# An attention layer's edge loop on one core: three product blocks per slot in place of four, and other PSUM banks

## What is computed

```python
w1 = rbf @ W_rbf
m1_s, m1_v = _cg_tp(msg_s, msg_v, y0, y1, ...)        # product 1
a = leaky(m1_s @ W_alpha).reshape(e, H, AS_);  a = sum(a * alpha_dot, -1)
ex = exp(a - amax[dst]);  alpha = ex / (den[dst] + 1e-16)
val_s = m1_s @ Ws_val
val_v = einsum('ecx,cd->edx', m1_v, Wv_val)
val_v = val_v * sigmoid(val_s @ Wg)[..., None];  val_s = sigmoid(val_s)
m2_s, m2_v = _cg_tp(val_s, val_v, y0, y1, ...)        # product 2
hs = m2_s @ Ws_vlin;  hv = einsum('ecx,cd->edx', m2_v, Wv_vlin)
agg = segment_sum(alpha * concat([hs, hv]), dst)
# _cg_tp: out_s = [w*s*y0, w*dot(v, y1)/sqrt3]
#         out_v = [(w*s)[:, :, None] * y1[:, None, :], w*v*y0, w*cross(v, y1)/sqrt2]
```

## Time and profile before

| | us |
|---|---|
| median of 3 runs | 13186.02 (13185.72 to 13264.55) |
| the profiled execution | 13248.87, its span 13246.9 |
| attention loop in that span | about 8588 to 13165 |
| one turn in the steady part | 10.00 on average |

### The profile page before, as it was taken

How to read it: one execution, slowest core, us unless ns; L and a number is a source line. 1 busy time by engine, 2 the same in 40 slices (tenths; PEclk the granted TensorE clock), 3 DMA queues, 4 the chain that set the end, 5 groups by cost and what they waited for, 6 DMA issues and landing times. The chain is left out here.

```text
span 13246.9 us, 282237 instructions
## 1 busy us (share of the span) xinstructions
PE 10905.0 (82%) x70500; PEld 7225.5 (55%) x70501; DVE 8435.5 (64%) x29911; ACT 4988.2 (38%) x15104; POOL 8742.7 (66%) x12926
## 2 busy tenths in 40 slices
PE   5454453588887999996999956599999999999998
PEld 2000000366664555554666622288888888888886
DVE  7555553499973334433332369588888888888886
ACT  0000000266541222221111100177777777777775
POOL 3777777466655567743777745277777777777775
PEclk9999999999987799985555568699999999999998
DMA  4101100133223233322333356100000000000000
GB/s 154 28 25 25 28 25 19 37 68 68 68 50 66 60 72 74 75 53 57 82 82 82 82 107 117 32 20 20 20 20 20 20 20 20 20 20 20 20 20 21
DMA packets 964724, 635.56 MB, mean 48 GB/s; under 512 B 702351, under 2 KB 886629, under 8 KB 960972
## 3 DMA queue, kind: packets, MB, share of 16 engines
q0 software_dynamic: 257120, 382.51, 11.7%
q1 hardware_dynamic: 691340, 204.27, 8.4%
q10 hardware_dynamic: 15776, 43.25, 0.8%
HBM read 543.06 MB, written 86.47 MB: 48 GB/s over the span
## 5 line engine op out<-in xcount | busy, mean ns | idle before, releaser
L1124 POOL DMA_INDIRECT l1s_node_rows<-node_table,l1s_edge_rows x1216 | 1236.0, 1016 | 655.1 <-issue 316.0
L1124 POOL DMA_INDIRECT l2s_node_rows<-node_table,l2s_edge_rows x1216 | 1152.5, 948 | 653.7 <-issue 351.8
L1209 PE MATMUL l1s_p_outer<-l1s_edge_by_node,l1s_node_rows 128*32 128x64 f32 (+2 forms) x14592 | 1248.9, 275 | 110.7 <-DMA l1s_node_rows<-node_table,l1s_edge_rows 94.0
L461 PE MATMUL rank<-onehot,lower_h 128*128 128x418 f16 x812 | 429.7, 529 | 1035.8 <-DVE onehot L437 966.2
L744 POOL DMA_INDIRECT l_source_rows<-node_table,l_edge_rows x928 | 939.8, 1013 | 437.3 <-issue 278.1
L1209 PE MATMUL l2s_p_outer<-l2s_edge_by_node,l2s_node_rows 128*64 128x40 f32 (+1 forms) x4864 | 1039.2, 345 | 152.8 <-DMA l2s_node_rows<-node_table,l2s_edge_rows 149.2
L1209 PEld LDWEIGHTS l2s_p_outer<-l2s_edge_by_node,l2s_node_rows 128*64 128x64 f32 (+1 forms) x4864 | 837.3, 233 | 549.9 <-issue 356.5
L1209 PEld LDWEIGHTS l1s_p_outer<-l1s_edge_by_node,l1s_node_rows 128*32 128x32 f32 (+2 forms) x14592 | 771.9, 132 | 668.9 <-issue 494.5
L474 POOL DMA_INDIRECT rows_by_src<-row_s,pos_i x812 | 846.6, 1043 | 416.4 <-issue 416.4
L1971 POOL DMA_INDIRECT l_source_rows<-node_table,l_edge_rows x914 | 891.1, 975 | 317.6 <-issue 244.4
L474 POOL DMA_INDIRECT rows_by_dst<-row_d,pos_i x812 | 845.0, 1041 | 267.3 <-issue 267.3
(11 more groups left out here) (504 smaller groups left out, 29142.2 us busy)
## 6 DMA issues: line engine op xcount, KB each, us to landing
l_xv_by<-h_turned_l SPq DMA_DIRECT2D x120, 320.0 KB, 10.6
l_source_rows<-node_table,l_edge_rows POOLq DMA_INDIRECT x1842
l_xs_by<-h_turned_l SPq DMA_DIRECT2D x40, 640.0 KB
rows_by_src<-pad_rows_s ACTq DMA_DIRECT2D x23, 1026.0 KB
l1s_edge_rows<-rows_by_src SPq DMA_DIRECT2D x304, 76.0 KB, 2.3
l2s_edge_rows<-rows_by_src SPq DMA_DIRECT2D x304, 76.0 KB, 2.5
l1s_node_rows<-node_table,l1s_edge_rows POOLq DMA_INDIRECT x1216
l2s_node_rows<-node_table,l2s_edge_rows POOLq DMA_INDIRECT x1216
```

The lines of the kernel that those rows point to most:

```text
L461: nc.tensor.matmul(rank[:, b, 0:BINS], K["lower_h"][:, :], onehot[:, b, :], start=True, stop=False)
L1124: pool.indirect_dma_start(xg[q][:, s, :], None, table, bass.IndirectOffsetOnAxis(ap=pay[q][:, s, S_DST:S_DST + 1].bitcast(U32), axis=0)).t ...
L1209: ins = nc.tensor.matmul(p_o[rows, j % RING, col:col + n], xg[q][:, s, lhs], rhs(eh[q % RING][:, s, :, :]), start=True, stop=True, skip_gr ...
```

## The change

Both products keep three blocks of 128 per slot in place of four. Block 0 holds the scalar outputs (96) and the third axis' share of one vector part (32 columns, the last third of the dot, which is no longer added on DVE but by the matmul, with the weight rows repeated). Block 1 holds the 64 scalars once, unscaled by `y1`, and the first two axes of `v*y0`; block 2 holds its third axis and the cross product of all three axes. The weights `w_v` and `w_hv` become [128, 2, 128]: 32 output columns for the projected scalar part, 96 for the three axes. The scalar part is multiplied by `y1` after the projection, on DVE (`spread`, `val_sum`; `head_spread`, `head_sum`), which the projection's linearity permits.

- PE: six transposes in place of eight, twice; per slot two 128-column matmuls in place of three of 96 columns, for values and for heads. `front_turn` is moved ahead of the transposes of `G_`. The values' matmuls now wait for this turn's `acc_done`, the heads' for `tanh_done`, the sums' for `val_made`.
- ACT: twelve scalings by `y1` go; copies have 384 columns; `gate` (tanh + 1), `sg` (tanh + 1, into `G_`) and four scalings by `y0` come. After `logits_done` the order is now alphas, tanh, gate, front copies, and only then the copies of `G_`.
- DVE: `us` goes straight into `F`; dots have two axes and one addition less; four spread and sum operations, and the head weighting in three pieces come. The order at the start of the turn is new.
- POOL: one small copy of `y1` more (`axis_kept`).
- PSUM: transposes and vector heads share two banks, logits and scalar heads one, values and node sums one.
- Set-up: 56 weight loads in place of 40.

The diff, cut to its core:

```diff
--- before.py
+++ after.py
@@ weights
-            n_loads, LOADS = [], 40
+            n_loads, LOADS = [], 56
@@ cross() on POOL
-                        TT(free(out[:, 0, 1, MS:MS + 1], [PT, PAIR], [P, 3], [1, CV]), there[:, :, :, :], back[:, :, :, :], ALU.subtract).then_inc(m[done], 1)
+                        TT(out[:, :, AT_X:PT].rearrange("p s (i c) -> p s i c", i=3), there[:, :, :, :], back[:, :, :, :], ALU.subtract).then_inc(m[done], 1)
@@ tensor
-                            for n in ("a_done", "a_scaled", "a_crossed"):
+                            for n in ("a_done", "a_crossed"):
                                 wait(n, -1)
-                            wait("g_copied", -1)
                             for s in range(PAIR):
-                                for c in range(4):
+                                for c in range(BLOCKS):
                                     ins = nc.tensor.transpose(...)
                                 ins.then_inc(m["f_turned"], 1)
                             wait("max_taken", 0, 1)
                             masked(1, prev2)
-                            wait("val_made", -1)
+                            wait("acc_done")
                             for s in range(PAIR):
                                 wait("f_copied", 0, s + 1)
...
-                                for i in range(3):
-                                    ins = nc.tensor.matmul(p_a[:, s, D:256], f_t[s][:, (i + 1) * P:(i + 2) * P], w_v[:, i, :], start=i == 0, stop=i == 2)
+                                for c in range(2):
+                                    ins = nc.tensor.matmul(values[:, s, :], f_t[s][:, (c + 1) * P:(c + 2) * P], w_v[:, c, :], start=c == 0, stop=c == 1)
                             ins.then_inc(m["logits_done"], 1)
+                            wait("a3_copied", -1)
+                            wait("hot_made")
+                            front_turn(ahead_u)
...
-                            wait("acc_done")
+                            wait("tanh_done")
                             for s in range(PAIR):
                                 wait("g_copied", 0, s + 1)
...
@@ scalar
                             wait("logits_done")
-                            wait("b_done", -1)
-                            nc.scalar.activation(slope[:, :, :], p_a[:, :, 0:CS], ACT.Copy, scale=0.2)
-                            nc.scalar.activation(th[:, :, :], p_a[:, :, CS:D], ACT.Tanh, scale=0.5).then_inc(m["tanh_done"], 1)
+                            wait("lsum_made", -1)
+                            nc.scalar.copy(alphas[:, :, :], logits[:, :, 0:CS]).then_inc(m["alphas_made"], 1)
+                            nc.scalar.activation(th[:, :, :], logits[:, :, CS:D], ACT.Tanh, scale=0.5).then_inc(m["tanh_done"], 1)
+                            wait("val_made", -1)
+                            wait("tanh_done")
+                            nc.scalar.add(gate[:, :, :], th[:, :, CS:MS], 1.0).then_inc(m["gate_made"], 1)
+                            wait("front_turned")
+                            wait("front_done", -1)
+                            front((u + 1) % 4)
                             wait("heads_done", -1)
                             for s in range(PAIR):
                                 wait("g_turned", 0, s + 1)
-                                nc.scalar.copy(g_t[s][:, :], p_t[s][:, :]).then_inc(m["g_copied"], 1)
-                            wait("front_turned")
-                            wait("front_done", -1)
-                            front((u + 1) % 4)
+                                nc.scalar.copy(g_t[s][:, :], p_t[:, s, 0:PT]).then_inc(m["g_copied"], 1)
@@ vector
+                            wait("shrink_done", -1)
+                            wait("acc_done", -1)
+                            shrunk = w.done(TT(acc_b, acc_b, ...shrink..., ALU.mult))
                             wait("front_done", -1)
                             msg_made = w.done(TT(msg[:, :, :], p_r[:, :, AT_DST:AT_DST + D], xg[u][:, :, :], ALU.add))
-                            wait("shrink_done", -1)
-                            wait("acc_done", -1)
-                            shrunk = w.done(TT(acc_b, acc_b, ...shrink..., ALU.mult))
+                            wait("summed", -1)
+                            w.after(shrunk)
+                            TT(acc_b, acc_b, p_sum..., ALU.add).then_inc(m["acc_done"], 1)
+                            onehot((u + 1) % 4, it * 16 + 16 * ((u + 1) // 4 + 1))
                             wait("f_turned", -1)
-                            wait("a_scaled", -1)
                             wait("a_crossed", -1)
                             w.after(msg_made)
-                            TT(us[:, :, :], p_r[:, :, CS:2 * CS], msg[:, :, 0:CS], ALU.mult).then_inc(m["us_made"], 1)
                             TT(uv[:, :, 1, :, :], weight(2), msg_v, ALU.mult).then_inc(m["ux_made"], 1)
                             v_made = w.done(TT(uv[:, :, 0, :, :], weight(1), msg_v, ALU.mult))
+                            TT(f[:, :, AT_SV:AT_V], p_r[:, :, CS:2 * CS], msg[:, :, 0:CS], ALU.mult)
+                            TT(by_axis(f[:, :, AT_V:AT_X]), weight(0), msg_v, ALU.mult)
+                            TT(f[:, :, 0:CS], p_r[:, :, 0:CS], msg[:, :, 0:CS], ALU.mult).then_inc(m["uv_made"], 1)
                             wait("masked", -1, 2)
                             nc.vector.tensor_reduce(qm[:, 0:2], p_m[:, :, :], AX.X, ALU.max).then_inc(m["max_taken"], 1)
-                            w.done(TT(parts(f, CS, CV), weight(0), msg_v, ALU.mult))
-                            TT(f[:, :, 0, 0:CS], p_r[:, :, 0:CS], msg[:, :, 0:CS], ALU.mult).then_inc(m["uv_made"], 1)
-                            wait("summed", -1)
-                            w.after(shrunk)
-                            TT(acc_b, acc_b, p_h[...SUM...], ALU.add).then_inc(m["acc_done"], 1)
...
                             wait("ex_done")
                             wait("heads_done")
-                            for s, done in ((0, "rows_used"), (1, "z_made")):
-                                TT(Z[:, s, :, 0:HW - 1], heads(s), ...weight..., ALU.mult).then_inc(m[done], 1)
+                            spread_made = w.done(TT(head_spread[:, :, :, :], ...p_t heads..., ...axis_kept..., ALU.mult))
+                            TT(Z[:, :, :, 0:AS], heads_s..., weigh([0, AS]), ALU.mult)
+                            w.after(spread_made)
+                            w.link(TT(head_sum[:, :, :, :], by_axis(head_v[:, :, CV:P]), head_spread[:, :, :, :], ALU.add))
+                            for s in range(PAIR):
+                                ins = TT(Z[:, s, :, AS:HW - 1]..., head_sum[:, s, :, :]..., ...weight..., ALU.mult)
+                            ins.then_inc(m["z_made"], 1)
```

More of the change, by code:

```diff
@@ L2174, in _ @@
                             nc.scalar.copy(a3_t[0:3 * HEADS, :], p_a3).then_inc(m["a3_copied"], 1)
-                            scale_b(1).then_inc(m["b_scaled"], 1)
+                            wait("val_made")
+                            for s in range(PAIR):
+                                ins = nc.scalar.activation(g[:, s, AT_V:AT_X], val_v[:, s, :, :].rearrange("p i c -> p (i c)"), ACT.Copy, scale=y0(s))
+                            ins.then_inc(m["b_scaled"], 1)
                 @block.vector
@@ new lines, in _ @@
+                            wait("max_made")
+                            TT(drop[:, :], top_b, mn[:, :], ALU.subtract).then_inc(m["drop_made"], 1)
+                            wait("drop_made")
+                            dve.sem_inc(m["dve_seen"], 1)
+                            nc.vector.tensor_copy(top_b, mn[:, :])
+                            wait("alphas_made")
+                            leaky_made = w.done(nc.vector.scalar_tensor_tensor(leaky[:, :, :], alphas[:, :, :], 0.2, alphas[:, :, :], ALU.mult, ALU.max))
@@ L2270, in _ @@
+                            spread_made = w.done(TT(spread[:, :, :, :], free(p_v[:, 0:1], [P, PAIR], [0, 3], [1, CV]), y1(prev, [1, 3], [0, CV]), ALU.mult))
                             wait("a3_made", -1)
@@ L2272, in _ @@
                             leaky_made = w.done(TT(leaky[:, :, :], leaky[:, :, :], free(alpha_dot[:, :], [0, PAIR], [1, CS]), ALU.mult))
-                            wait("b_crossed", -1)
-                            wait("sg_made")
-                            TT(val_v[:, :, :, :], free(sg[:, 0, CS:CS + 1], [MS, PAIR], [0, 3], [1, CV]),
-                               p_a[:, :, D:256].rearrange("p s (i c) -> p s i c", i=3), ALU.mult).then_inc(m["val_made"], 1)
+                            w.after(spread_made)
+                            val_summed = w.done(TT(val_sum[:, :, :, :], by_axis(values[:, :, CV:P]), spread[:, :, :, :], ALU.add))
                             w.after(leaky_made)
@@ L2282, in _ @@
                             TT(ea[:, :, :], logit[u % 2][:, :, :], p_r[:, :, AT_MAX:AT_MAX + HEADS], ALU.subtract).then_inc(m["ea_made"], 1)
-                            g = G_[prev % 2]
```

(10 more changed lines are left out.)

198 lines of the change are left out of this document (103 added, 95 removed).

## The result

| | before | changed |
|---|---|---|
| median of the runs on one chip | 13187.35 us | 13658.64 (13574.6 to 13705.86, 4 runs) |
| ratio, 95% interval | | 1.0336 (1.0272 to 1.0399) |
| profiled execution, its span | 13248.87, 13246.9 | 13647.27, 13645.3 |
| one turn in the steady part | 10.00 | 10.81 |

What follows compares the result with a forecast made beforehand. It took a ring of engine hand-offs, not PE's work, as the bound: 10.62 us plus 0.12 for loop ends made 10.74 a turn; 456 turns × 0.74 plus 12 set-up gave 349 over 13186, about 13535 us (12980 to 13780).

Steps and rivals of the forecast that it cites:

- The ring: Engines hand each attention-loop turn round in a chain, forecast to grow from 9.89 to 10.62 us; chance 0.67.
- six pieces: Parts of one turn's chain between engines, forecast at 4.34, 0.82, 2.05, 1.70, 0.16 and 1.55 us.
- Piece 1: From heads done on PE to DVE's first max read: 4.34 us forecast, 3.03 before.
- the head weighting: DVE's two last weightings after the head sum, starting at 1.01 and 1.18 us, about 0.25 each.
- The 0.19 of waiting for the sums: After forming the message, until 2.29 us, DVE would wait 0.19 for PE's sums, ready at 2.48.
- 128 columns cost as 4: PE's 128-column records would take 0.112 us each, columns being free below some width; bounds 0.11 and 0.14.
- Loop ends: Ends of hardware loop passes would cost 0.5 us per pass, 0.12 a turn; bounds 0 and 0.6 per pass.
- Set-up: Sixteen more weight loads at 0.49 us of SP's queue each: 8 us, 12 with landing.
- Whoever takes work from PE gains at most 0.26 us a turn until the ring is shortened too: Before the change, the chain was 9.63 us without its 0.26 of slack, PE's own work just above it.
- the clock: Rival: the added order costs and PE's clock falls too, +4.4 us a turn, about 15500 us; chance 0.04.
- Piece 4: From the end of the values to ACT's first copy of product 2: 1.70 us forecast, 1.12 before.
- a turn of 9.9: Rival: gains and costs nearly cancel, turn 9.9 to 10.2 us, 13130 to 13290 us; chance 0.12.

Runs made afterwards that it cites:

- (1): Changed kernel with DVE's first max read moved up, ahead of the three products into F: 13247.11 us, ratio 1.0056.
- run 9: Changed kernel with GpSimd's cross product of product 2 done on 2 of 32 channels, the rest left out: 13482.42 us, ratio 1.0194.
- run 8: Kernel before with three of four blocks transposed and copied, two of three multiplied, the third axis left out: 13194.4 us, ratio 0.9993.
- both_early: Changed kernel with DVE's first max read ahead of the products into F and ACT's copies of product 2 directly behind tanh: 13227.41 us, ratio 1.0005.
- before_read_late: Kernel before with DVE's first max read placed behind its products, the sums' addition and the one-hot: 13550.26 us, ratio 1.0261.
- run 7: Kernel before with ACT's front copies placed ahead of the copies of product 2: 14618.39 us, ratio 1.107.
- ring_short: Changed kernel reordered: DVE's message, weighted_v, rescaling, read first, one-hot behind the second read, register loads behind product 2; ACT's product 2 copies early: 13566.64 us, ratio 1.0292.
- run 2: Changed kernel with ACT's copies of product 2 directly behind tanh, ahead of the gate and front copies: 13587.01 us, ratio 1.0295.
- run 3: Changed kernel with both moves, DVE's first max read early and ACT's copies of product 2 directly behind tanh: 13227.41 us, ratio 1.0005.
- 5: ring_short with the one-hot moved back behind the sums, directly after the first max read: 13368.09 us, ratio 1.0145.
- dots2_on_act: both_early with one register load fewer, both products' axis weightings on ACT and the read directly behind the sums' addition: 12982.96 us, ratio 0.9807.

## Why the prediction was right, and where not

**The ring was the right picture.** Five of six pieces are within 0.02; moving the read gives 0.7 us a turn in the changed kernel (1) and, with the one-hot, takes 0.85 in the one before (6).

**The time is 124 us over the forecast.** 34 of that are the loop (371 in place of 337). Most of the rest is the base: the forecast started at the median before, 13186, but the profiled run that it read lies 63 above that, and between the two profiled runs the difference is 398, not 471. Beside the later runs the kernel before had medians of 13199 to 13250.

**Piece 1 was 0.20 too short** (the mean turn, 10.81, is 0.07 over the forecast's 10.74). The term mis-sized is the head weighting, "about 0.25" each: the two take 0.63 where 0.42 was worked out, and on average 0.355 each. The rescaling, put at 0.61, takes that on average (0.606) but 0.71 in this turn. The forecast knew of such stretching and left it to the range; it belonged in the sum, since both lie in the ring, and run 9 shows that GpSimd's multiplications lengthen both. The Trainium skill, page "SBUF — State Buffer", section "Who interferes with whom", says which: a VectorE instruction with both inputs in SBUF contends with GpSimd's reads, one with at most one, outside the page's two-port modes, does not. Runs here agree: L2325 and L2247 (two SBUF inputs) stretch and give it back in cross_cut, and L2250 (one input in PSUM) takes 0.48 in either.

**The 0.19 of waiting for the sums**: in this turn the message ends at 11014.98 and the sums' addition starts at 11015.01. The longer rescaling took the place of the wait, so the two errors cancel in part.

**128 columns cost as 4.** Taken as 0.112; measured starts lie 0.11 apart and four records take 0.61 to 0.66. The gap by columns of the Trainium skill, page "TensorE: Matmul & The Clock Gate", section "Back-to-back issue gap", did not hold here, as forecast. The Trainium skill, same page, section "LDWEIGHTS (loading the stationary operand)", gives 1/1.2 ns for each weight column; for 128 that is an estimate of 107 ns. The rows from 4 to 128 moving columns fit it; four records of 164 columns take 0.64 from start to start (11014.08 to 11014.72) and do not.

**Loop ends** were put at 0.12 a turn and hardly show: the mean turn (10.81) is that of the turn read (10.84), and the four turns of a pass average 10.64 to 11.01, where before one of four took 10.52 and the others 9.72 to 9.91. **Set-up** was 12 and is 6.

**"Whoever takes work from PE gains at most 0.26 us a turn until the ring is shortened too"**: run 8 gained 0.19 at full clock, but not for that reason. Its cut takes some 0.9 out of the ring as well, and what then holds the turn is DVE's list, a path that the forecast did not weigh; that the number fits is luck. In time it gained nothing, because the clock fell in one turn of five. The forecast gave the clock 0.04 and had no way to say when. PE idles 22% of the loop in the changed kernel, 17% in both_early and 10% in before_read_late, all at 1.00; it idles 9% in 7 and 8, whose clock fell, but 18% in ring_short, where it fell too. The idle share doesn't tell the two apart.

**Piece 4 was weighed wrong.** Its length is right; that its 0.58 more over before are all paid is not (run 2: 0.06). The ring was summed as if it were the only one. Pieces 1 and 4 taken together give all back (run 3), piece 1 alone 0.71 of 0.77.

**Two of the rivals' sums are loose**: a turn of 9.9 gives 13186 - 46 + 12 = 13152, not 13130, and the ring's own bounds add up to 10.2 to 11.6 a turn, not 10.3 to 11.5. The forecast hangs on neither.

**Not shown**: why the clock falls in 4, 5, 7 and 8 and in no turn of the changed kernel. Wait before the fall and length of PE's full stretches both differ between them, and no run changed one alone.

## What to carry to other kernels

Where engines hand work round in a ring, the busiest engine's work is not the price list: find the ring, and ask of each instruction moved into it whether the next engine needs it; here three DVE products ahead of a read cost 0.7 us a turn while 1.4 us less of PE's busy time brought none of it back. Look for the second and third ring before promising a gain: here each step gave 0.06 to 0.2 us before the next one held. Work that a loop no longer does pays only where its engine's list is the bound. Of all that was tried, only taking work off DVE came out ahead of the kernel before: a register load left out (0.25%), then weightings moved to ACT, which waits at that place (1.9% in all).

## What was unexpected of the hardware

- The clock can alternate within a turn, in five turns of six (run 7): 0.50 for 6.8 us that begin 1.7 us after a wait of 1.14, full for the rest. With that, an order worth about 1 us costs 3.1 a turn.
- A register load takes 0.31 us in DVE's list, with 0.06 for its register step, nearly a product of 192 elements (0.35).
- Removing work can lengthen what is left. A DVE copy of 4 elements per partition takes 0.17 in the changed kernel's turn and 0.45 in dots2_on_act (busy, mean ns):

```profile
L2298 DVE COPY l_maxima<-l_new_max 128x4 f32 x409 | 182.2, 445 | 62.2 <-DVE l_max_step L2295 62.2
```

It has one input, so it isn't one of the two-input instructions above; whether GpSimd holds it up, and with what, was not tried.
